# Sixteen blocks ahead of the last scatters, dense block outputs, and gathers that accumulate, in a recurrence followed by a mixture of experts

## The reference

```python
x = x + recurrence(layernorm(x), W_in, b_in, W_gx, b_gx, W_ga, b_ga, a_real, a_imag, W_out, b_out)
x = x + experts(layernorm(x), gate_w, w11, w33, w22, sw1, sw2, sw3)

# recurrence: xh = x@W_in + b_in; sigmoid gates by block-diagonal products;
# complex a and inputs from them; h[t] = a[t]*h[t-1] + xc[t] over the 512 tokens; out = [h.re, h.im]@W_out + b_out

# experts
scores = sigmoid(xf @ gate_w.T)                  # 2048 tokens x 32 experts
# the 4 best of 8 groups of 4 experts, in them the 6 best experts
w = scores[idx] / sum(scores[idx]) * 2.5
c = zeros(T, 32).at[token, idx].add(w)
g = einsum('td,eid->tei', xf, w11); u = einsum('td,eid->tei', xf, w33)
y = einsum('tei,te,edi->td', silu(g) * u, c, w22)
shared = silu(xf @ sw1.T) * (xf @ sw3.T) @ sw2.T
return (y + shared).reshape(x.shape)
```

## Time and profile before

| | us |
|---|---|
| median of 3 runs | 448.93 (447.82 to 449.15) |
| the profiled execution, its own time | 450.83 |
| its span | 449.1 |
| PE busy in the span | 376.1 (84%) |
| DVE busy | 294.3 (66%) |
| ACT busy | 260.7 (58%) |
| POOL busy | 231.6 (52%) |

### The profile page before, as it was taken

How to read it: one execution, slowest core, us unless ns; L and a number is a source line. 1 busy time by engine, 2 the same in 40 slices (tenths; PEclk the granted TensorE clock), 3 DMA queues, 4 the chain that set the end, 5 groups by cost and what they waited for, 6 DMA issues and landing times.

```text
span 449.1 us, 9145 instructions
## 1 busy us (share of the span) xinstructions
PE 376.1 (84%) x2120; PEld 301.2 (67%) x2121; DVE 294.3 (66%) x990; ACT 260.7 (58%) x585; POOL 231.6 (52%) x242
## 2 busy tenths in 40 slices
PE   2777696965976778399889999999999998998935
PEld 2644263745645563155579999999999997997924
DVE  3669688999988824612235555555567777777982
ACT  2678978768575132011157777767777776776710
POOL 2000000752778777777516666666656665663750
PEclk9898867595785687689999999999999999999996
DMA  8990000220335999333347666666689889879724
GB/s 241 405 339 2 0 0 1 74 102 15 118 118 201 413 430 380 130 128 128 117 145 215 188 195 182 204 188 191 191 265 354 255 248 300 303 208 336 244 83 174
DMA packets 41850, 87.70 MB, mean 195 GB/s; under 512 B 7204, under 2 KB 32295, under 8 KB 41296
## 3 DMA queue, kind: packets, MB, share of 16 engines
q1 hardware_dynamic: 28384, 54.77, 36.7%
q0 software_dynamic: 10704, 30.07, 18.6%
q10 hardware_dynamic: 2720, 2.40, 1.7%
HBM read 49.81 MB, written 39.71 MB: 199 GB/s over the span
## 4 chain that ended last, share of the span: by engine, by line
PE 50%; DVE 19%; ACT 9%; DMA 8%; issue 8%; POOL 3%; DVEq 1%; SPq 1%; ACTq 0%; POOLq 0%
PE PS L1228 17%; PE PS L1235 8%; PE PS L1165 7%; DMA payload_and_xn_t<-choice_rows 5%; PE PS L1220 4%; PE PS L1121 3%; POOL choice_rows L441 3%; PE PS L1178 3%; DMA resid<-in_x 2%; PE PS L1076 2%; ACT L605 1%; DVE st L682 1%; PE PS L1261 1%; ACT payload_and_xn_t L555 1%; DMA choice_rows<-block_out_s,block_meta 1%
## 5 line engine op out<-in xcount | busy, mean ns | idle before, releaser
L441 POOL DMA_INDIRECT choice_rows<-block_out_s,block_meta x127 | 127.0, 1000 | 86.0 <-issue 58.3
L427 POOL DMA_INDIRECT bucket_rows<-payload_and_xn_t,dest x96 | 101.9, 1062 | 116.2 <-DVE dest L874 88.2
L1228 PE MATMUL PS<-block_rows_t,block_gate_up_weights 128*128 128x128 f32 x1016 | 134.9, 276 | 0.0
L1228 PEld LDWEIGHTS PS<-block_rows_t,block_gate_up_weights 128*128 128x128 f32 x1016 | 123.4, 192 | 1.1 <-ACT block_rows_t L630 0.9
L625 ACT ACTIVATE block_gate_up_weights<-expert_weights 128x512 f32 x127 | 80.0, 630 | 35.6 <-issue 29.6
L1235 PE MATMUL PS<-expert_weights,block_hidden_t 128*128 x254 | 76.3, 382 | 3.8 <-DVE block_hidden_t L985 3.8
L992 DVE TENSOR_SCALAR block_out_s<-PS,block_meta 128x256 f32<-128x256 f32 x127 | 61.2, 482 | 0.0
L985 DVE TENSOR_TENSOR block_hidden_t<-block_silu_t,PS 128x128 f32<-128x128 f32 x127 | 36.3, 286 | 24.2 <-ACT block_silu_t L617 22.0
L630 ACT ACTIVATE block_rows_t<-PS 128x256 f32<-128x256 f32 x127 | 46.5, 366 | 7.6 <-PE PS L1220 7.6
L1220 PE MATMUL PS<-ident,block_rows_s 128*128 128x128 f32 x254 | 48.6, 273 | 1.4 <-DVE resid L964 1.3
L980 DVE COPY block_meta<-block_rows_s 128x2 f32 x127 | 22.0, 173 | 41.7 <-issue 41.4
(11 more groups left out here) (185 smaller groups left out, 459.1 us busy)
## 6 DMA issues: line engine op xcount, KB each, us to landing
block_rows_s<-bucket_rows SPq DMA_DIRECT2D x127, 160.0 KB
payload_and_xn_t<-choice_rows SPq DMA_DIRECT2D x16, 768.0 KB, 6.5
bucket_rows<-pad_rows SPq DMA_DIRECT2D x1, 5120.0 KB, 26.3
expert_weights<-in_experts SPq DMA_DIRECT2D x1, 4224.0 KB, 14.0
expert_weights<-in_experts SPq DMA_DIRECT2D x1, 3456.0 KB, 16.3
expert_weights<-in_experts SPq DMA_DIRECT2D x1, 2688.0 KB, 18.3
resid<-in_x SPq DMA_DIRECT2D x4, 512.0 KB, 9.3
choice_rows<-block_out_s,block_meta POOLq DMA_INDIRECT x127, 3.2
```

Of the source, the lines that this page charges most:

```text
L427: nc.gpsimd.indirect_dma_start(out=bucket_ap[:, :], out_offset=bass.IndirectOffsetOnAxis(ap=dest[:, t, k:k + 1], axis=0), in_=PAY[:, t, :] ...
L441: nc.gpsimd.indirect_dma_start(out=choice_ap[0:rows, :], out_offset=bass.IndirectOffsetOnAxis(ap=meta_id[:, slot, 1:2], axis=0), in_=yy[:, ...
L1228: ins = mm(PS[:, 2 + r, g * P:(g + 1) * P], ws[:, r, (2 * k + g) * P:(2 * k + g + 1) * P], xT[:, r, k * P:(k + 1) * P], start=(k == 0), st ...
```

## The change

*Rows.* A bucket row is 288 wide, one weight per expert and no row numbers; L855 and L857 are gone. `dpos`, the bucket places, is kept for all 16 tiles.

*The table.* Phases are cut finer, nine instead of five, so the table's columns are 288 wide instead of 160, and it has four quantities instead of three. A small table of the first 16 blocks (`early_blocks`), full blocks of the first eight tiles only, is made by 22 operations on DVE right after the last `places`; the main table is made among the shared expert's hidden rows, and its four transposes stand on PE behind the fourth gate and up product. After it DVE works out for each token where its six results will lie (`output_rows`, `output_sources`).

*Loads and stores.* SP first writes zeros over the buffer of the block outputs, in five parts during the recurrence. It loads the 16 early blocks when the first three chunks are scattered, and from then on writes each block's output densely to `bucket_outputs`, 11 blocks behind the loads. It also stores all tiles.

*The way back.* POOL scatters nothing in the loop. When the blocks of a tile are written it gathers six times per tile, 128 rows each, into three sums: sum 0 is the tile of `resid` itself, sums 1 and 2 are buffers. Four of the six gathers add in the transfer. DVE adds sums 1 and 2 to `resid`, two additions per tile. Tiles run in order from 0 to 15.

*Loops.* The engines' loops are unrolled by 8 (`LP`): PE and ACT take 14 turns of it, and DVE has a second loop form with the additions.

The diff, cut to what the text speaks of:

```diff
-    ROW = D + 2 * E
+    ROW = D + E
-    NMETA = 16
-    LP = 16
+    NMETA = 8
+    LP = 8
-    PHASE_ENDS = (1, 2, 3, 4, 5)
+    CUTS = [[2], [2], [2, 4], [2, 4], [2], [1, 2]]
+    LOOPED = BLOCKS // LP * LP
+    RING = 4
+    SUMS = 3
+    EARLY_BLOCKS = 16
+    EARLY_TILES = 8
+    FIRST_ADD = 67
+    FIRST_STORE = 80
+    WRITE_LAG = NXS + 3
...
         @block.sync
+            for n in range(NCH - 1):
+                part = slice(n * BLOCKS // (NCH - 1), (n + 1) * BLOCKS // (NCH - 1))
+                sp.wait_ge(s_gp, n + 1)
+                sp.dma_start(outputs_ap[part.start * P:part.stop * P]..., PADT[:, 0:D]...).then_inc(s_clear, 16)
...
-                row = sp.value_load(tabs[0:1, bass.ds(j, 1)], min_val=0, max_val=E * CAP - P)
-                sp.dma_start(xs[:, slot, :], bucket_ap[bass.ds(row, P), :]).then_inc(s_xs[slot], 16)
-            def load_choices(n):
-                all_scattered(sp, blocks_through(phase_of(n)))
-                ...
-                sp.dma_start(RINGS[:, n % RING].rearrange("p k d -> p (k d)"), choice_t[NT - 1 - n]).then_inc(s_cin[n], 16)
+            def load_block(j, u, taken):
+                if u % 4 == 0:
+                    sp.reg_load(first_rows, tabs[0:1, bass.ds(j, 4)])
+                ...
+                row = sp.snap(first_rows[u % 4], min_val=0, max_val=PLANE - P)
+                sp.dma_start(xs[:, u % NXS, :], bucket_ap[bass.ds(row, P), :]).then_inc(s_xs[u % NXS], 16)
+            def write_block(j, u):
+                if u % 4 == 0:
+                    sp.reg_load(first_outputs, tabs[0:1, bass.ds(j + 3 * P, 4)])
+                sp.wait_ge(s_y, j + 1)
+                row = sp.snap(first_outputs[u % 4], min_val=0, max_val=2 * P * P - P)
+                sp.dma_start(outputs_ap[bass.ds(row, P), :], yy[:, u % NY, :]).then_inc(s_ys[u % NY], 16)
+            rows_scattered(0, early_chunks)
+            for j in range(EARLY_BLOCKS):
+                load_block(j, j, j - NXS + 1 if j >= NXS else None)
+                if j >= WRITE_LAG:
+                    write_block(j - WRITE_LAG, j - WRITE_LAG)
+            rows_scattered(early_chunks, NCH)
...
         @block.gpsimd
-            def scatter(j, slot, ready, rows):
-                pool.wait_ge(s_y, ready)
-                ...
+            def gather_outputs(n):
+                all_written(pool, blocks_through(phase_of(n)))
+                pool.wait_ge(s_src, n // TS + 1)
+                if n < RING:
+                    pool.wait_ge(s_resid, B)
+                if n >= RING:
+                    pool.wait_ge(s_added, added(n - RING))
+                for k in range(TOPK):
+                    part = k % SUMS
+                    landed = s_cin[n % RING][part]
+                    into = resid[:, n, :] if part == 0 else RINGS[:, n % RING, part - 1, :]
+                    if k >= SUMS:
+                        pool.wait_ge(landed, 16 * (TOPK // SUMS) * (n // RING) + 16)
+                    nc.gpsimd.indirect_dma_start(
+                        out=into, out_offset=None, in_=outputs_ap[0:BLOCKS * P, :],
+                        in_offset=bass.IndirectOffsetOnAxis(ap=source[:, n, k:k + 1], axis=0),
+                        compute_op=ALU.add if part == 0 or k >= SUMS else ALU.bypass).then_inc(landed, 16)
...
         @block.vector
-                c.add(V.tensor_tensor_scan(rank[:, n, :]..., flat_memb, flat_memb, 0.0, AD, ALU.bypass))
-                c.wait()
-                c.add(STT(PAY_id[:, rows, D + 1::2], rank[:, n, :], ...))
...
-                    (ln2_stats, 5), (ln2_shift, 5), (choose, 4), (choose, 5), (places, 4), (places, 5)):
+                    (ln2_stats, 5), (ln2_shift, 5), (choose, 4), (choose, 5), (places, 4), (places, 5), (early_blocks, 0)):
...
+            def add_sum(n, k, turn=None):
+                ...
+                TT(total, total, RINGS[:, slot, k, :], AD).then_inc(s_added, 1)
...
         @block.tensor
             shared_gate_up(0, 0)
+            positions(4)
+            positions(5)
             pe.wait_ge(s_xn2, NCH)
             shared_gate_up(0, 1)
-            positions(4)
-            positions(5)
-            pe.wait_ge(s_dest, NCH)
-            pe.wait_ge(s_tabf, 3)
-            mm(PS[0:1, 3, 0:P], tabf[:, 3:4], ident[:], start=True, stop=True)
...
+            shared_gate_up(1, 0)
             for b in range(B):
-                if b + 1 < B:
+                if 0 < b and b + 1 < B:
                     shared_gate_up(b + 1, 0)
                 shared_down(b)
                 if b + 1 < B:
                     shared_gate_up(b + 1, 1)
+                if b == 0:
+                    block_table()
```

More of the change, by code:

```diff
@@ L962, in shared_out, with output_sources @@
+            def output_sources(g):
+                at_least(dve, s_src, g)
+                dve.wait_ge(s_added, 1)
+                for t in range(TS):
+                    c.add(V.max(dv[:, t, :], dpos[:, g * TS + t, :]))
+                c.wait()
+                TSC(source[:, g * TS:(g + 1) * TS, :], dv[:, :, 0:TOPK], -1.0, None, AD).then_inc(s_src, 1)
             def shared_out(b):
@@ L1024, in _, with add_at @@
+            def add_at(u, turn=None):
+                tile, k = u // (2 * TOPK) * 2 + u % (2 * TOPK) // ADDS, u % ADDS
+                if u % (2 * TOPK) < 2 * ADDS:
+                    add_sum(tile, k, turn)
+            for s in range(LP + 3):
                 step(s, s)
-            with dve.Fori(LP, UNROLL_AT, LP) as i:
+            with dve.Fori(LP + 3, FIRST_ADD, LP) as i:
                 for u in range(LP):
-                    step(i + u, u)
-            for s in range(UNROLL_AT, BLOCKS + 2):
-                step(s, s)
-                for n in range(NT):
-                    if n in ADD_AT and ADD_AT[n] <= s < ADD_AT[n] + TOPK // ADD_RATE[n]:
-                        for _ in range(ADD_RATE[n]):
-                            add_choice(*divmod(adds["done"], TOPK))
@@ L1034, in _ @@
-            while adds["done"] < PE_SUM * TOPK:
-                add_choice(*divmod(adds["done"], TOPK))
-            for k in range(TOPK):
-                add_choice(NT - 1, k)
+                    step(i + u, u + 3)
+            with dve.Fori(0, ADD_TURNS, 1) as turn:
+                for u in range(ADD_STEPS):
+                    step(turn * ADD_STEPS + (FIRST_ADD + u), FIRST_ADD + u)
+                    add_at(u, turn)
+            for u in range(ADD_TURNS * ADD_STEPS, BLOCKS + 2 - FIRST_ADD):
+                step(FIRST_ADD + u, FIRST_ADD + u)
+                add_at(u)
@@ L1040, in _ @@
+            done = sum(u % (2 * TOPK) < 2 * ADDS for u in range(BLOCKS + 2 - FIRST_ADD))
+            for m in range(done, NT * ADDS):
+                add_sum(*divmod(m, ADDS))
         @block.tensor
@@ L1180, in shared_down, with block_table @@
                 ins.then_inc(s_shyp, 1)
+            def block_table():
+                pe.wait_ge(s_dest, NCH)
+                pe.wait_ge(s_tabf, 3)
+                for q in range(4):
+                    ins = mm(PS[0:1, 3, q * P:(q + 1) * P], tabf[:, 6 + q:7 + q], ident[:], start=True, stop=True)
+                ins.then_inc(s_tabp, 1)
             pe.wait_ge(s_shw, 32)
```

442 lines of the change are left out of this document (251 added, 191 removed).

## The result

The changed kernel takes 485.65 us (484.73 to 487.43), the kernel before 448.94 in the same comparison: ratio 1.0828, 95% interval 1.0791 to 1.0865. The forecast was 444.8, the range 440.5 to 462.0. The profiled execution has a span of 482.9 us, 33.8 longer than before's 449.1.

A forecast was written before the change was run, and what follows sets the result against it. DVE was taken to bound the recurrence and PE the loop of 127 blocks. Router -1.5, table -4.6, loop -2.3 and tail +4.3 sum to -4.1: span 445.0, median 444.8 us, range 440.5 to 462.

The forecast's parts named there:

- its first rival: Way back: adding gathers are dear and POOL becomes the bound, 467 us at 1.5 times the price, 493 at twice; chance 0.16.
- The step that failed: Way back: POOL's six gathers per tile each cost what a bucket scatter does, one every 1.26 us, 7.8 us per tile.
- the point of decision: Way back: above 9.3 us per tile, half of the 18.5 us between pairs of tiles, POOL becomes the bound.
- Its own formula: Dear gathers: loop start 222.3, plus 83 to the first gather, plus 16 times a tile's time, plus 5; 9.8 gives 467.
- costs two plain ones: Way back: upper bound for the price of one adding gather on POOL, given as 2.2.
- The overlap: Way back: a pair of tiles takes 15.6 of 18.5 us, so POOL waits for blocks until the last four tiles.
- The reason against the rival: Against dear gathers: 0.96 us is the preparing of 128 rows, and the row count is the same.
- The loop: Loop over blocks: PE's 3.8 us of waits go, 1.5 for more loop turns comes in; -2.3, ends -3.8 and -0.7.
- The front: Ahead of the loop: router -1.5 and table -4.6, so the loop starts at 222.3 instead of 228.4.
- SP as the bound: Rival in the loop: SP needs 1.65 us per block and becomes the bound, +10, 455 us; chance 0.07.
- The zeros written in front: Recurrence: 16.6 MB of zeros to the output buffer between 45 and 140 us, put at no cost.
- The tail: From the last down product to the end: 21.9 us instead of 17.6, +4.3, with four tiles left for POOL.

The follow-up runs named there:

- e1_noadd: The changed kernel with none of its 96 gathers adding in the transfer, half of each token's expert results left out; 461.69 us, ratio 1.0269.
- e6_pairs: The changed kernel with the gathers of two tiles interleaved, first three of each, then the adding three of each; 473.87 us, ratio 1.0572.
- e5_half: The changed kernel with only half of each block's output row written and gathered, 512 instead of 1024 bytes, as many rows; 475.05 us, one execution.
- e2_plain6: The changed kernel with six plain gathers per tile into six buffers and six additions per tile on DVE; 452.31 us, ratio 1.0086.
- e3_unroll: The changed kernel with DVE's loop of 24 steps written out, its additions kept; 485.16 us, ratio 1.083.
- e4_late: The changed kernel with SP waiting for all six chunks' scatters before the first block load; 491.54 us, ratio 1.0957.
- e7_cuts: e2_plain6 with a tenth phase that ends at tile 13 and block outputs written 9 instead of 11 blocks behind the loads; 446.09 us, ratio 0.9938.
- e9: e1_noadd with eight more DVE steps written out ahead of its first loop; gap at the branch 0.26 us, on a slow chip, no time given.
- e14: The kernel of e9 run a second time; gap at the branch 0.26 us, again on a slow chip, no time given.
- e17: The kernel of e9 run a third time, where the kernel before took 449.2 us; 453.58 us, one execution.
- e8: e2_plain6 with DVE's first loop, which adds nothing, 32 steps long, and additions and stores moved back; 465.39 us, one execution.

## Why the prediction was wrong

It named the right mechanism, as its first rival, with 0.16, and put the likeliest value of its price too low. Span by span, forecast and measured against before: the loop's start -6.1 and -6.1; from there to the end of the last down product -2.3 and +9.1; from there to the end +4.3 and +30.8.

*The step that failed* is "at that price, with a little for the ten waits ahead of a tile, it takes 6 x 1.26 + 0.2 = 7.8 us". Four of the six take 1.53 to 1.60 instead of 0.96 (4 x 0.6 = 2.4 us, e1_noadd), and the landing is 4.8 us in the middle instead of 2.5, so that the fourth gather waits up to 2.2 (e6_pairs). A tile took 10.7 on average, (474.43 + 1.85 - 305.60) / 16, above the 9.3 that the prediction gave as the point of decision. Its own formula then gives 222.3 + 83 + 16 x 10.7 + 5 = 481.5; measured 482.9. The bound "costs two plain ones" (1.92) held the value; the fault was to take the lower neighbour because it was the only row. The overlap fell with it: POOL was to wait for blocks until the last four tiles, and from 305.60 on its only waits were for its own first gathers to land. The reason against the rival, that 0.96 us is the preparing of 128 rows and their count is the same, was half right: e5_half shows that rows and not bytes count, but an adding row counts for 1.6 plain ones.

The Trainium skill (Collectives: The Full Stack, The bandwidth ceiling: the fold count and why AG ≠ RS ≠ AR) says of an add in the transfer of a collective that it has a read descriptor for each of two sources. The direction agrees: 1.58 for 0.95 in e1_noadd, the same for half the bytes in e5_half. The size does not follow from it, since POOL's time is 1.6 times and not twice, and the packets of POOL's queue are three times as many, one per row and not one per four rows. That POOL's time goes by descriptors is not shown; no row counts them. The forecast had cited the rule and left the rival at 0.16.

*The loop.* By itself the new loop is what was forecast: 195.46 us in e2_plain6 for 199.06, a gain of 3.6, at the good end of the range, since 14 turns of the 8-step loops cost PE 0.1 in a few places, where 1.5 was put in. In the changed kernel it lost 13 us against that. Of these 5.4 and 1.7 lie at the turn of DVE's 24-step loop, a term that the sum did not have: it priced turns from the earlier trace rows by their number and not by where their code lies. Another 7 are small steps under full DMA engines (e5_half). None of it moved the end, since POOL was the bound from 305.6 on, and e3_unroll, without the turn, takes as long.

*The front.* Forecast and measured: third product 183.2 less the router's gain, and 181.75; start of the loop 222.3, and 222.28. The parts differ little: the early table took 4.6 instead of 5.3, the router gave 1.1 instead of 1.5, and the clock at 0.68 for 5.3 us loses the 1.7 that were forecast. e4_late shows that the leading blocks carry 4.5 of the 6.1 us.

*SP as the bound* did not come: SP waited 45.0 us in the loop, 22.9 of it at the start, for DVE to take blocks that were loaded ahead. The zeros written in front delayed nothing that the start of the loop shows.

*The tail.* 21.9 us were forecast for 7.8 us per tile. e2_plain6 has that price and still 29.2, for two reasons. Its last four tiles open 3.8 us later than the sum had them (189.0 for 185.2 after the loop's start): the write of block 114 is issued 1.8 later and takes over 4 us to land, not 2.5. And from the start of the last gather to the end it takes 10.1 us, where the sum had 5.6; the changed kernel takes 8.5 there. Landing and addition take 3.2 of the 10.1 and the last store's packets 1.4; the rest is POOL's end (e7_cuts), a term that the sum did not have and that no version mends. That e7_cuts comes near 21.9 with 23.5 is luck in part: its last gather starts 3.0 us earlier than forecast, and its end takes 4.5 longer.

## What to carry to other kernels

Where the decision point lies inside the interval of a price without a row of its own, give each side a chance by its share of the interval, and not by the nearest row: here 9.3 us per tile means 1.35 us per adding gather, and over half of the interval from 0.96 to 1.92 lies above it. Moving additions from a half-idle DVE (0.42 us each) into the transfers of the engine that was next to be the bound (0.6 us more each, and a landing to wait for) is a bad trade; six plain gathers and 96 additions beat it by 33 us. Look in the trace behind each long loop's branch: a turn can cost 5 us or 0.3, depending on where its code lies.

## What the runs showed of the hardware

- An adding gather of 128 rows occupies POOL 1.53 to 1.60 us, a plain one 0.94 to 1.01 in most cases; the median of those into `resid` is 1.574 at 1024 bytes per row (the changed kernel) and 1.576 at 512 (e5_half). It moves its rows in 128 packets, a plain one in 32 of 4096 bytes.
- The turn of one loop of 24 steps cost DVE 4.3 to 5.6 us in five kernels (the changed one, e1, e4, e5, e6) and 0.3 when 8 more steps of straight code stood ahead of it (e9, e14, e17); a body of 32 steps elsewhere cost 0.3 (e8). The Trainium skill (Runtime: NRT & Kernel Launch, Instruction fetch mechanics) says that a taken branch whose target lies outside the two pages of code at hand has to wait for a load of it. The two or three instruction transfers inside each wait, and none in e17's gap, agree; that 32 steps turned without one is not explained by length alone, and which pages were at hand no run here shows.
- A block write landed after 3.2 us in the middle and 4.6 at the most in the changed kernel (2.9 and 5.3 in e1_noadd), a gather after 4.8 in the middle, where a bucket scatter landed after 2.5.
- From the end of its last gather to the end of its closing instruction POOL took 8.9 us in e7_cuts and 6.8 in the changed kernel, 5.3 and 2.6 us beyond the last packet of the last store.
